# Layer 0's edge stage: one-hots stored in pairs, the running maximum spread between the halves of the weighing, row waits by halves

## The chip, the cores and the metric

The kernel runs on one core of a Trainium2 chip. The metric is the device time of one execution in microseconds (us). Engines are called by their short names in the profile: PE is TensorE (PEld its loading of weights), DVE VectorE, ACT ScalarE, POOL GpSimd, SP SyncE. The granted TensorE clock has two levels, 1.2 and 2.4 GHz; the profile writes it as a share, 0.50 and 1.00.

## What is computed

A graph network of four layers over 6250 nodes of 128 features and 206250 edges. Only layer 0's edges are touched by the change. Cut to that layer:

```python
def _L0_gnn_ref(x, edge_index, W_w, W_b, a_w, a_b):
    h = x @ W_w + W_b
    row, col = (edge_index[0], edge_index[1])
    e = h[row] @ a_src + h[col] @ a_dst + a_b
    e = jax.nn.leaky_relu(e, negative_slope=0.01)
    attention = jax.nn.softmax(e, axis=0)          # over all edges at once
    msg = attention * h[col]
    return jax.ops.segment_sum(msg, row, num_segments=N_NODES)
```

The softmax runs over all edges, so the kernel keeps one running maximum and rescales the sums when it rises.

## The kernel before

The edges are sorted by source and cut into tiles of 128, one edge to a partition; a pair of tiles belongs to one block of 128 nodes. `l0_edges` goes through them in units of 32 tiles (`U`), which fall into two halves of 16 tiles (8 pairs). There are 54 units. The loops over them (one on each engine) have a body of six units. Three row buffers (`R`) take turns; SyncE refills one half at a time once its sums are made (`summed`) and its locations saved (`saved`).

A row has 128 features, a one, the destination's part of the score, the edge's location in its block (column W - 2) and its index. For a unit n, the engines share the work so:

- **VectorE** compares the location with 0..127 (`compare`, L1248), one half of a unit at a time: `sel`, 128 columns of zeros and a one for each tile, in bf16. It works out the scores (`finalize`, from L1255: sum of the three parts, bias, leaky relu, the partition's maximum into `mx`), takes the maximum over the partitions (`raise_max`, L1263 and L1264, into `mrun`), renews the negated maximum (`renew`, L1271 and L1273), multiplies the one-hots by the weights `p` (`weigh`, L1279, two halves, into `oh`, f32), and adds the 16 pair sums to `agg` (`add`, L1290); which block is added to is read from memory into registers, for eight pairs at a time (L1116).
- **TensorE** transposes the one-hots (`turn`, L1179, four groups of eight tiles), multiplies them with the source's score parts (`score`, L1186), turns `mx` (`turn_max`, L1192), spreads `mrun` to all partitions (`spread_out`, L1196), and makes the pair sums (`total`, L1206): 16 f32 multiplies of 129 columns for a half, which the profile shows as 32 records.
- **ScalarE** copies each transposed group out of PSUM (`evacuate`, L1144; there is one such buffer), makes the exponentials (`exponents`, L1148 and L1149), scales `agg` (L1161), and saves locations and indices (L1165, L1166).

All orders are written out by hand. In the step of unit n, VectorE does `weigh(n)` in both halves, `compare` of unit n+2's first half, `raise_max(n+1)`, `compare` of the second half, `renew(n+1)`, `add(n)`, `finalize(n+2)`. TensorE does `turn_max(n+1)`, `total(n)` for the first half, the first `turn` of n+2, `spread_out(n+1)`, half of `total(n)` for the second half, the second `turn`, the first `score`, the other half of the second `total`, and the remaining turns and scores, the last of which releases `finalize(n+2)`. Each engine takes its instructions in this order. There is one buffer of weighed one-hots (`oh`), one place in PSUM for each half's sums (`psA`), and two buffers of `sel`.

## Time and profile before

| | us |
|---|---|
| median of 3 runs | 12102.42 |
| lowest, highest | 12091.43, 12109.16 |
| the profiled execution | 12107.04 |
| its span, first to last instruction | 12105.2 |
| layer 0's edge stage in it, first to last weighing | 3340.3 to 4367.8 |

The whole kernel is a row of stages; the stage that matters here is 1/12 of it. The page's averages over the span say little of it, so the rows below come from questions to the trace about this stretch. In the timeline, rows of one kind that follow each other are merged, and the brackets tell how long the engine stood idle before the row, and what it waited for. "issue" is idle time for which the profile shows no wait.

### The profile page before, as it was taken

To read this page: it belongs to the slowest core of one execution; us is meant where nothing else is said; L and a number is where in the kernel's file an instruction comes from. 1 tells how busy PE (TensorE), PEld (TensorE's weight loads), DVE (VectorE), ACT (ScalarE), POOL (GpSimd) and SP (SyncE) were. 2 spreads that over 40 slices of the span, in tenths; PEclk is the share of its full clock that TensorE was granted. 3 is DMA by queue.
4 is the path that set the end of the run, shared out by engine and by line. 5 is a ranking of instruction groups with operands and counts; after the bars stand their busy time and mean duration, and the time that the engine had idled before them with its cause. 6 is when DMAs were issued, how large, how long until landed. Compare 5 with 4: busy or idle time off the path is not lost. (4 is left out here: it accounts for less than half of the span.)

```text
span 12105.2 us, 161778 instructions
## 1 busy us (share of the span) xinstructions
PE 7567.7 (63%) x46439; PEld 6355.7 (53%) x46440; DVE 6295.9 (52%) x14477; ACT 2657.0 (22%) x4442; POOL 5226.8 (43%) x5267
## 2 busy tenths in 40 slices
PE   3433333333266647777777772999956777777775
PEld 2233333333266645555555552666636777777775
DVE  8722222222277765555555554777764555555555
ACT  4011111111155541111111112444420000000000
POOL 0166666666500016666666662000015555555553
PEclk7766666666677778888888886999975555555555
DMA  4144444443444434444444453000012222233225
GB/s 142 49 126 126 125 126 127 127 125 125 139 109 109 115 101 121 116 123 119 121 124 116 123 112 76 0 0 0 0 36 73 81 80 80 80 82 82 80 81 80
DMA packets 1150557, 1137.58 MB, mean 94 GB/s; under 512 B 239363, under 2 KB 959825, under 8 KB 1150117
## 3 DMA queue, kind: packets, MB, share of 16 engines
q1 hardware_dynamic: 948422, 666.82, 19.0%
q0 software_dynamic: 195904, 465.66, 14.7%
q10 hardware_dynamic: 6048, 2.84, 0.1%
q8 instruction: 93, 1.52, 0.1%
q14 instruction: 90, 0.74, 0.0%
HBM read 731.30 MB, written 403.51 MB: 94 GB/s over the span
## 5 line engine op out<-in xcount | busy, mean ns | idle before, releaser
L1051 POOL DMA_INDIRECT buf<-node_rows,buf x1728 | 1716.9, 994 | 1218.8 <-issue 1033.2
L1545 POOL DMA_INDIRECT buf<-node_rows_ln,buf x1728 | 1751.6, 1014 | 1088.0 <-DVE buf L1672 596.7
L717 POOL DMA_INDIRECT edge_rows_by_src<-buf x1728 | 1695.1, 981 | 1080.8 <-ACT buf L727 537.0
L761 PE MATMUL psum<-buf 128*128 x3456 | 725.5, 377 | 1714.1 <-ACT buf L736 1089.8
L761 PEld LDWEIGHTS psum<-buf 128*128 128x128 f32 x3456 | 656.0, 282 | 1769.9 <-issue 1769.1
L2437 PE MATMUL psum<-buf 128*128 128x132 f32 x3456 | 886.0, 412 | 479.2 <-issue 469.1
L2437 PEld LDWEIGHTS psum<-buf 128*128 128x128 f32 x3456 | 774.0, 309 | 564.5 <-issue 562.9
L2048 PE MATMUL psum<-parts,buf 128*128 x4896 | 917.6, 329 | 99.8 <-DVE buf L2084 44.8
L2429 PE MATMUL psum<-buf 128*128 128x5 f32 x3456 | 754.8, 356 | 164.7 <-ACT buf L2406 83.1
L2429 PEld LDWEIGHTS psum<-buf 128*128 128x128 f32 x3456 | 745.2, 332 | 180.3 <-ACT buf L2406 93.2
L1670 DVE TENSOR_TENSOR buf<-psum,buf 128x512 f32<-128x512 f32 x432 | 298.1, 690 | 1014.6 <-remote 679.2
L2064 DVE TENSOR_TENSOR buf<-buf,ends_of 128x2048 bf16<-128x2048 bf16 x616 | 727.1, 1222 | 124.4 <-issue 120.9
L2026 ACT CAST buf<-psum 128x1024 bf16<-128x1024 f32 x612 | 619.5, 1012 | 693.5 <-PE psum L2037 693.5
L1602 PE MATMUL psum<-buf 128*128 128x512 f32 x864 | 563.0, 739 | 295.5 <-ACT buf L1563 267.9
L809 DVE COPY buf<-buf 128x32 int32<-128x32 int32 x108 | 23.1, 214 | 1368.2 <-DMA buf<-records_by_dst 1127.8
L1560 ACT ACTIVATE buf<-psum 128x512 f32<-128x512 f32 x432 | 258.0, 597 | 2052.3 <-remote 1157.4
L1607 PEld LDWEIGHTS psum<-buf 128*128 128x128 f32 x3456 | 546.3, 224 | 282.8 <-issue 282.8
L2048 PEld LDWEIGHTS psum<-parts,buf 128*128 128x128 bf16 x4896 | 471.9, 96 | 411.6 <-issue 204.4
L2199 POOL IOTA buf<- 49x1 f32 x1 | 0.1, 125 | 1464.1 <-POOLq L844 1464.1
L727 ACT COPY buf<-psum 128x520 f32<-128x520 f32 x432 | 248.9, 595 | 1675.1 <-remote 1217.8
L1615 PE MATMUL psum<-buf 128*128 128x128 f32 x3456 | 518.5, 297 | 132.4 <-DVE buf L1672 101.1
L1206 PE MATMUL psum<-buf 128*128 128x129 f32 x3456 | 538.2, 324 | 100.8 <-DVE buf L1279 100.8
(430 smaller groups left out, 13911.4 us busy)
## 6 DMA issues: line engine op xcount, KB each, us to landing
buf<-edge_rows_by_src SPq DMA_DIRECT2D x114, 1056.0 KB, 5.7
buf<-edge_rows_by_src SPq DMA_DIRECT2D x110, 1024.0 KB
buf<-in_edge_attr SPq DMA_DIRECT2D x864, 128.0 KB
running_weighted_sums<-buf SPq DMA_DIRECT2D x108, 544.0 KB
buf<-loc_rows_by_src SPq DMA_DIRECT2D x110, 512.0 KB
buf<-loc_rows_by_dst SPq DMA_DIRECT2D x110, 512.0 KB
running_sums<-buf SPq DMA_DIRECT2D x108, 512.0 KB
edge_rows_by_src<-buf SPq DMA_DIRECT2D x139, 260.0 KB, 2.8
```

Source lines behind the costliest of these rows:

```text
L717: nc.gpsimd.indirect_dma_start(rows, bass.IndirectOffsetOnAxis(ap=at[:, h, t:t + 1], axis=0), st[:, h, t, :], None).then_inc(scattered[h], 16)
L761: last = nc.tensor.matmul(psX[:, g % 2, t // 2, (t % 2) * WT:(t % 2 + 1) * WT], ohT[:, g % 2, t * P:(t + 1) * P], flat(tab[:, bass.ds(bloc ...
L1051: nc.gpsimd.indirect_dma_start(rows[:, t, 0:used], None, table, bass.IndirectOffsetOnAxis(ap=stage[:, t:t + 1], axis=0)).then_inc(sem, 16)
L1206: last = nc.tensor.matmul(psA[:, half, q // 3, (q % 3) * W:(q % 3) * W + D + 1], oh[:, t, :], rows[:, s, t, 0:D + 1], start=(k == 0), stop ...
L1545: nc.gpsimd.indirect_dma_start(xn[:, j, t, :], None, table1, bass.IndirectOffsetOnAxis(ap=stage[:, j // 4, at:at + 1], axis=0)).then_inc(g ...
L1602: nc.tensor.matmul(psH[:, 0], w1[:], sT[:, j % 2], start=True, stop=True).then_inc(h_ps, 1)
L1607: last = nc.tensor.matmul(psT[:, (j + 1) % 2, t * P:(t + 1) * P], hS[:, (j + 1) % 2, t * P:(t + 1) * P], w2[:], start=True, stop=True)
L2026: nc.scalar.copy(meets[:, h % 2].rearrange("p a k -> p (a k)"), psM[:, h % 2].rearrange("p a k -> p (a k)")).then_inc(moved, 1)
L2048: last = nc.tensor.matmul(psO[:, h // 2, 0:3 * XW], meets[:, h % 2, k, :], parts[:, bass.ds(blocks[k], 1), :, :].rearrange("p b w d -> p ( ...
L2064: last = nc.vector.tensor_tensor(to[:, b], bc(iota[:].unsqueeze(1), [P, U // 2, P, 2]), bc(ends_of[:, w, at].rearrange("p (a t) -> p a t", ...
L2429: last = nc.tensor.matmul(psS[:, q, :], oh[:, s, 2 * q + k, :], sel[:, b, 2 * q + k, :], start=(k == 0), stop=(k == 1))
L2437: last = nc.tensor.matmul(sums(q), oh[:, h, 2 * q + k, :], rows[:, h, 2 * q + k, :], start=(k == 0), stop=(k == 1))
```

## The change

It touches `l0_edges` alone.

1. `sel`, `oh` and `iota` are stored with two tiles interleaved: [.., pair, 128, 2] and no longer [.., tile, 128]. Transposes and sums read one tile as every second element. A new instruction on VectorE (`pick`, L1251 of the kernel after) copies 16 locations at a time into a bf16 array `locs`, and `compare` takes its locations from there, in pairs, so all its operands are bf16. `weigh` reads `p` in pairs.
2. VectorE's order in a step is now: first half of `weigh(n)`, `raise_max(n+1)`, second half, `renew(n+1)`, then `pick` and `compare` twice, then `add` and `finalize`.
3. TensorE spreads the maximum ahead of all sums of the unit. The second half sum is cut into 3 and 5 pairs, not 4 and 4, and the first 3 tell VectorE (`partly`) that they are made; `add` waits for the rest before its fourth pair.
4. Each half of a row buffer has a semaphore of its own.

```diff
-        rows, oh = sb([P, R, U, W]), sb([P, U, P])
-        sel, turned_sel = sb([P, 2, U, P], BF16), sb([P, GROUPS_U, TURN, P], BF16)
-        iota, ident = sb([P, P], BF16), sb([P, P], BF16)
+        rows, oh = sb([P, R, U, W]), sb([P, U // 2, P, 2])
+        sel, turned_sel = sb([P, 2, U // 2, P, 2], BF16), sb([P, GROUPS_U, TURN, P], BF16)
+        iota, ident, locs = sb([P, P, 2], BF16), sb([P, P], BF16), sb([P, 2, U], BF16)
...
-                        act.wait_ge(got[u % R], 64 * i + 32 * (u // R) + 32)
                         for half in range(2):
+                            act.wait_ge(got[u % R][half], 32 * i + 16 * (u // R) + 16)
...
-                        last = nc.tensor.transpose(psT[:, t, :], sel[:, k, TURN * g + t, :], ident[:])
+                        at = TURN * g + t
+                        last = nc.tensor.transpose(psT[:, t, :], sel[:, k, at // 2, :, at % 2], ident[:])
...
-                            last = nc.tensor.matmul(psA[:, half, q // 3, (q % 3) * W:(q % 3) * W + D + 1], oh[:, t, :], rows[:, s, t, 0:D + 1],
+                            last = nc.tensor.matmul(psA[:, half, q // 3, (q % 3) * W:(q % 3) * W + D + 1], oh[:, t // 2, :, t % 2], rows[:, s, t, 0:D + 1],
...
                     if whole:
                         turn_max(n + 1)
+                        spread_out(n + 1)
                         total(n, s, 0, range(PAIRS))
                     turn(n + 2, k, 0)
                     blocks = blocks_of(ENG.PE, first_pair)
                     if whole:
-                        spread_out(n + 1)
-                        total(n, s, 1, range(PAIRS // 2))
+                        total(n, s, 1, range(3))
                     turn(n + 2, k, 1)
                     score(n + 2, 0, blocks)
                     if whole:
-                        total(n, s, 1, range(PAIRS // 2, PAIRS))
+                        total(n, s, 1, range(3, PAIRS))
...
+                def pick(n, half, k, s, halves_at):
+                    dve.wait_ge(got[s][half], halves_at)
+                    of = slice(half * HALF, (half + 1) * HALF)
+                    nc.vector.tensor_copy(locs[:, k, of].unsqueeze(2), rows[:, s, of, W - 2:W - 1]).then_inc(picked, 1)
+
+                def compare(n, half, k, weighed=None):
+                    dve.wait_ge(picked, 2 * n + (half + 1))
                     if weighed is not None:
                         dve.wait_ge(weighted, 2 * weighed + (half + 1))
...
+                    nc.vector.tensor_tensor(sel[:, k, of], bc(iota[:].unsqueeze(1), [P, PAIRS, P, 2]), bc(by_two(locs[:, k, half * HALF:(half + 1) * HALF]), [P, PAIRS, P, 2]),
                                             ALU.is_equal).then_inc(hot, 1)
...
+                    nc.vector.tensor_tensor(oh[:, at], sel[:, k, at], bc(by_two(p[:, k, of]), [P, PAIRS, P, 2]), ALU.mult).then_inc(weighted, 1)
...
-                        dve.wait_ge(summed, 2 * n + (half + 1))
                         for q in range(PAIRS):
+                            if q == 0 and half == 1:
+                                dve.wait_ge(partly, n + 1)
+                            elif q == 3 * half:
+                                dve.wait_ge(summed, 2 * n + (half + 1))
...
-                        weigh(n, u % 2)
-                        compare(0, u % 2, (u + 2) % R, rows_at, n)
+                        halves_at = 32 * i + 16 * ((u + 2) // R + 1)
+                        weigh(n, u % 2, 0)
                         raise_max(n + 1)
-                        compare(1, u % 2, (u + 2) % R, rows_at, n)
+                        weigh(n, u % 2, 1)
                         renew(n + 1)
+                        for half in range(2):
+                            pick(n + 2, half, u % 2, (u + 2) % R, halves_at)
+                            compare(n + 2, half, u % 2, n)
                         add(n, i * (4 * R * PAIRS) + 2 * u * PAIRS, i * (4 * R * PAIRS) + 2 * u * PAIRS)
```

How it moves instructions, first on VectorE, in the loop's second unit, from the weighing on. ISA and REGISTER_ALU are steps of the engine's sequencer. Before:

```order
L1279 TENSOR_TENSOR buf<-buf 128x2048 x2
L1244 REGISTER_ALU
L1246 ISA
L1248 TENSOR_TENSOR buf<-buf 128x2048
L1263 TENSOR_REDUCE buf<-psum 1x1
L90 REGISTER_ALU
L1264 TENSOR_TENSOR buf<-buf 1x1
L1246 REGISTER_ALU
L1248 TENSOR_TENSOR buf<-buf 128x2048
```

And after (L1289 is the weighing, L1273 and L1274 the maximum, L1281 and L1283 the renewal, L1251 the new copy, L1258 the comparison):

```order
L1289 TENSOR_TENSOR buf<-buf 128x2048
L1273 TENSOR_REDUCE buf<-psum 1x1
L90 REGISTER_ALU
L1274 TENSOR_TENSOR buf<-buf 1x1
L1289 TENSOR_TENSOR buf<-buf 128x2048
L1281 TENSOR_SCALAR buf<-buf 128x1
L1282 REGISTER_ALU
L1283 TENSOR_SCALAR buf<-psum 128x1
L1249 REGISTER_ALU
L1251 CAST buf<-buf 128x16
L1254 ISA
L1256 ISA
```

The maximum stands between the weighings, and the comparison comes behind the renewal, with a copy and a wait of its own ahead of it.

On TensorE, at the head of the step of a unit within the loop, L1192 turns the maximum, L1196 spreads it, L1206 are the sums and L1179 the transposes. Before:

```order
L1192 MATMUL psum<-buf 1x128
L1206 MATMUL psum<-buf 128x129 x16
L1176 ISA
L1177 REGISTER_ALU
L1179 MATMUL psum<-buf 128x128 x8
L1116 ISA
L1116 TENSOR_LOAD buf
L1196 MATMUL psum<-buf 128x1
L1206 MATMUL psum<-buf 128x129 x8
```

After (L1194, L1198, L1208 and L1181 in the same roles):

```order
L1194 MATMUL psum<-buf 1x128
L1198 MATMUL psum<-buf 128x1
L1208 MATMUL psum<-buf 128x129 x16
L1177 ISA
L1178 REGISTER_ALU
L1181 MATMUL psum<-buf 128x128 x8
L1116 ISA
L1116 TENSOR_LOAD buf
L1208 MATMUL psum<-buf 128x129 x6
```

The spread moved from behind the first transposes to ahead of the first sum, and the sum behind the transposes has six multiplies for eight.

## Rows read from the trace of the kernel before

**Rows 1.** The weighing, L1279, by line: count, durations in ns, idle time before it

```profile
L1279 DVE TENSOR_TENSOR buf<-buf x108: 2281/2284/2293, 3340.3 to 4367.8; 128x2048 f32<-128x2048 bf16 x108
...
  issue: 25.1, 8
```

**Rows 2.** Groups by line and shape, 3340 to 4366 us: busy us, mean ns | idle

```profile
L1290 DVE TENSOR_TENSOR agg<-agg,psum 128x129 f32 x848 | 246.9, 291 | 194.4 <-issue 54.4 <-DVE agg L1290 36.7
L1248 DVE TENSOR_TENSOR buf<-buf 128x2048 bf16<-128x2048 bf16 x106 | 242.6, 2289 | 0.0
...
L1179 PE MATMUL psum<-buf 128*128 128x128 bf16 x1696 | 129.8, 219 | 49.0 <-ACT buf L1144 49.0
```

**Rows 3.** Timeline, one unit: start us, duration us, engine, line, names, [idle]

```profile
3747.57 4.48 DVE L1279 TENSOR_TENSOR buf<-buf 128x2048 f32<-128x2048 bf16 x2
...
3749.90 5.47 PE L1206 MATMUL psum<-buf 128*128 128x129 f32 x32 [1.83 <-DVE buf L1279]
3751.97 2.29 DVE L1248 TENSOR_TENSOR buf<-buf 128x2048 bf16<-128x2048 bf16 x1
...
3754.47 0.15 DVE L1264 TENSOR_TENSOR buf<-buf 1x1 f32<-1x1 f32 x1
3754.57 2.29 DVE L1248 TENSOR_TENSOR buf<-buf 128x2048 bf16<-128x2048 bf16 x1
...
3755.21 0.61 PE L1179 MATMUL psum<-buf 128*128 128x128 bf16 x8
...
3755.75 0.38 PE L1196 MATMUL psum<-buf 1*128 1x1 f32 x2
...
3756.05 2.05 PE L1206 MATMUL psum<-buf 128*128 128x129 f32 x16
...
3756.96 0.16 DVE L1273 TENSOR_SCALAR buf<-psum 128x1 f32<-128x1 f32 x1
...
3757.98 3.33 DVE L1290 TENSOR_TENSOR agg<-agg,psum 128x129 f32 x8 [0.86 <-issue]
...
3762.11 2.46 DVE L1290 TENSOR_TENSOR agg<-agg,psum 128x129 f32 x6 [0.80 <-DVE agg L1290]
...
3763.99 0.61 PE L1186 MATMUL psum<-buf 128*128 x8 [1.02 <-ACT buf L1144]
...
3765.49 0.25 DVE L1255 TENSOR_REDUCE buf<-psum 128x32 f32<-128x96 f32 x1
3765.61 5.69 ACT L1161 ACTIVATE agg<-agg,buf 128x6468 f32<-128x6468 f32 x1 [1.76 <-DVE agg L1290]
```

**Rows 4.** Timeline, the unit after it

```profile
3766.41 4.48 DVE L1279 TENSOR_TENSOR buf<-buf 128x2048 f32<-128x2048 bf16 x2
...
3768.75 6.25 PE L1206 MATMUL psum<-buf 128*128 128x129 f32 x32 [1.82 <-DVE buf L1279]
...
3780.98 3.32 DVE L1290 TENSOR_TENSOR agg<-agg,psum 128x129 f32 x8 [0.66 <-DVE agg L1290]
...
3783.62 0.62 PE L1186 MATMUL psum<-buf 128*128 x8 [1.02 <-ACT buf L1144]
3784.28 0.26 DVE L1255 TENSOR_REDUCE buf<-psum 128x32 f32<-128x96 f32 x1
```

**Rows 5.** Busy time by window: us, PE, PEld, DVE, ACT, POOL, PEclk, DMA, GB/s

```profile
3753.20:3755.30 2.10, 2.10 (x21) 2.09 (x20) 2.07 (x4) 0.00 (x0) 0.00 (x0) 0.97 0.00 0
3772.20:3773.70 1.50, 1.50 (x9) 1.50 (x9) 1.47 (x4) 0.00 (x0) 0.00 (x0) 0.50 0.00 0
```

**Rows 6.** Layer 2's comparison, L2064, by line: min/median/max ns

```profile
L2064 DVE TENSOR_TENSOR buf<-buf,ends_of x616: 1216/1222/1227, 7558.4 to 8862.4; 128x2048 bf16<-128x2048 bf16 x154
```

**Rows 7.** Loading of block numbers by VectorE's sequencer, L1116: min/median/max ns

```profile
L1116 DVEq TENSOR_LOAD <-buf x108: 594/600/881, 3349.9 to 4379.1; - x108
```

**Rows 8.** Timeline, the first comparison of the stage

```profile
3312.71 4.49 DVE L1248 TENSOR_TENSOR buf<-buf 128x2048 bf16<-128x2048 bf16 x2 [4.98 <-DMA buf<-edge_rows_by_src]
```

**Rows 9.** Layer 2's multiplies of bf16 one-hots in pairs, L2037: min/median/max ns

```profile
L2037 PE MATMUL psum<-buf x4904: 217/218/314, 7560.8 to 8862.4; 128*128 128x128 bf16 x197
```

More of the change, by code:

```diff
@@ L1306, in _ @@
                 renew(0, again=False)
-                compare(0, 1, 1, 32)
-                compare(1, 1, 1, 32)
+                for half in range(2):
+                    pick(1, half, 1, 1, 16)
+                    compare(1, half, 1)
                 finalize(1, 1, 1)
```

39 lines of the change are left out of this document (19 added, 20 removed).

## Prediction

> **What bounds the kernel now.** Only layer 0's edge stage is edited, so I read that stage alone. The weighing's row gives its borders: the first weighing starts at 3340.3, the 108th at 4367.8 us [rows 1]. That is 54 units with two weighings each; the last unit starts one weighing (2.2) before 4367.8, so 53 periods fill 4365.6 - 3340.3 = 1025.3 us, 19.35 each. Eight of them cross the end of the loop's body of six units; there VectorE stands for 25.1 us in all [rows 1]. The rest is (1025.3 - 25.1) / 53 = 18.87 us for a unit.
>
> The groups by line say what VectorE does in a unit: two weighings of 2.28, two comparisons of 2.29, sixteen additions of 0.29 [rows 2]. The timeline of one unit then shows which wait ends last. I count from the start of its weighing, 3747.57 [rows 3]. TensorE's first half sum (below: T0) starts at 2.33, when the first weighed half is ready, and takes 5.47. Then come eight transposes, the spread of the maximum (L1196), half of the second sum, and so on in a row to the last scores, which end at 3764.60, or 17.03. VectorE goes weigh, weigh, compare, maximum, compare, renew (ends 3757.12), 0.86 us of loading block numbers, eight additions, 0.80 us of the same, eight additions. `finalize` follows them without idle time, at 3765.49, or 17.92. So in this unit VectorE is last, and TensorE's chain has ended 0.89 us earlier.
>
> The next unit [rows 4] starts at 3766.41 and reads differently: T0 takes 6.25, the scores end at 3784.24 (17.83), the additions at 3784.30 (17.89). Both chains end together. The cause is TensorE's clock: in the first unit it is at 0.97 from 3753.2 on, 3.3 us after T0 began; in the second it is still at 0.50, the lower of the two levels, up to 3773.7, 4.95 us after T0 began [rows 5]. The two sorts take turns nearly throughout: by T0's length 28 of the 54 units are long (5.9 or more) and 26 short. **The point of the whole case:** VectorE is the bound by 0.9 us in every other unit and by nothing in the others.
>
> From finalize's start to the next weighing it is 0.92 (3765.49 to 3766.41), and finalize starts about 0.05 after the last scores where it waits for them. TensorE's chain alone would thus give a period of 17.03 + 0.97 = 18.00 in the short sort, 17.83 + 0.97 = 18.80 in the long one.
>
> **VectorE's side of the change.** Each comparison becomes all bf16, in pairs. The same form stands in layer 2: 128x2048 bf16 in 1222 ns [rows 6], against 2289 [rows 2]. Two of them: -2.13 us. Added are two copies of 16 location values. The nearest rows are VectorE's one-element 0.16 (L1273) and small L1264, 0.15 [rows 3]; with the comparison's wait for each I take 0.3 each, +0.6. The block numbers' load, 594 to 600 ns [rows 7], and the 0.86 us around it follow the renewal's 0.16 us instruction today; behind the second comparison (1.22 us) they are hidden: -0.8. If that cover is absent, 0.8 comes back, still below TensorE's end. The weighing stays a mix of bf16 and f32; I leave it at 2.28.
> New chain: weighing 2.20, maximum 0.40, weighing 2.20 (the steps in [rows 3]: 4.40 for the pair, 2.60 for comparison and maximum), renewal 0.35, copies and comparisons 0.6 + 2.4, so 8.15 instead of 10.41 for the first addition. From there to finalize it was 7.5 (3757.98 to 3765.49), so VectorE could be there at 15.65 and have a period near 16.6: 2.2 us less. Were VectorE alone, that is 54 x 2.2 = 119 us.
>
> **TensorE's side.** T0 now stands behind the spread of the maximum, and that waits for the maximum, which follows the first weighing. The first weighing is done at 2.20, L1264 ends 0.45 later (it ends at 3754.62, and the comparison ahead of it gave way at 3751.97 + 2.20 = 3754.17), TensorE needs 0.05 to see it, and from the spread to the next sum it is 0.30 (3755.75 to 3756.05) at full clock, some 0.1 more at the low one. T0 starts at 3.0 to 3.1 and not at 2.33: +0.7. In return the spread leaves the place between transposes and second sum: these are 0.84 apart now (3755.21 to 3756.05), eight transposes alone cost about 0.45, so -0.4. T0's first multiply also finds its weights loaded behind the spread, which may give up to 0.15. Net +0.3, bounds +0.1 and +0.5. The 3+5 split of the second half sum adds no work. The first transposes of the new unit need a comparison done at about 6.7, as late as today (3751.97 + 2.29 = 6.69) and before T0's end near 8.5. The first additions now wait for T0 (8.5 or 9.3), and end at 16.1 or 16.9: 1.2 us before the scores (17.3 or 18.1). The wait at the fourth addition for the whole second half costs nothing then. ScalarE's scaling of agg (5.69 us, from 3765.61) starts earlier and stays hidden. SyncE's loads follow `summed` and `saved` as before.
> So **the wait that goes (finalize on the additions) is replaced by another one (finalize on the scores)**. Period: 18.0 + 0.3 = 18.3 in a short unit, 18.8 + 0.3 = 19.1 in a long one, mean 18.7. With a less favourable low-clock stretch I take 18.75, 0.1 below the 18.87 of now: 54 x 0.1 = -5 us. TensorE's quiet time ahead of T0 is 4.1 us in every unit (0.97 + 3.1); today it is 4.1 or 3.3 and the clock is at 0.50 at T0's start in both sorts, so I expect no unit without the drop.
>
> **Start of the stage.** The first comparison waits for both halves of the rows (4.98 us of idle time [rows 8]); now for one. The four turns behind it are paced by ScalarE, so only the first comparison's 1.07 less 0.3 counts, twice: -1.5, and perhaps 0.5 for the earlier half. -2 us. The loop's crossings (25.1 us) stay.
>
> **Stride.** The sums now read their f32 weights from every second element, the transposes theirs in bf16. Layer 2 multiplies such bf16 operands at 218 ns [rows 9], the transposes here take 219 [rows 2]: nothing. No row has f32 weights at such a step. I take nothing; the bound is a rival below.
> The Trainium skill, page "SBUF — State Buffer", section "Door 1: The DMA port swizzle", says that SBUF is read at full bandwidth while at least two accesses fall on one line of 16 bytes. f32 at every second element has exactly two, so by it the sum is unchanged, while one less would make this change slower. No run here shows it yet.
>
> **Sum.** -5 - 2 = -7 us on the profiled execution's 12107.0 (span 12105.2), so 12100. That execution is 4.6 us above the median of the three runs, 12102.4; the same -7 on the median is 12095.5.
>
> **Rivals.**
> (a) The low clock lasts long in every unit. T0 starts later against the clock's rise, and all units are of the long sort or longer: 19.1 to 19.4, so 0.25 to 0.5 x 54 = +13 to +28 us. It decides from a T0 of 6.2 us in nearly every unit. For it: units with 6.25 exist and TensorE now has no slack to hide them. Against: short units exist as well and the period hardly moves. 0.12, half of that past 0.2%.
> (b) f32 weights at a step of two load slower. At full clock a record of T0's kind takes 2.05 / 16 = 0.13 us; if loading took twice as long as the stream, 64 records a unit cost up to 0.1 us more each, 6.4 x 54 = +350 us. It shows as a longer mean of the sums' multiplies than now. For it: no row covers the form. 0.08.
> (c) Short units in a row: 18.3 each, 0.55 x 54 = -30 us. Needs the clock's rise to fall well in every unit. 0.08.
> (d) The clock stays up between units, so T0 takes 4.1 (twice 2.05), TensorE's period is 18.3 - 1.4 = 16.9, and VectorE's gain comes through: -1.9 x 54 = -100 us. Against it: 3.3 us of quiet lose the clock today. 0.05.
> (e) The comparison does not get faster (form not taken at two elements a cycle). VectorE's period is then 16.6 + 2.1 = 18.7: no more than TensorE's mean, +5 us. 0.03.
>
> **How the numbers follow.** My forecast has 0.64, plus (e) and half of (a) that stay within 0.2% (24 us, about what a measurement of this kernel can tell from no change): same 0.72. Faster: (d) 0.05, (c) 0.08 and a little of the forecast's fast edge, 0.14. Slower: (b) 0.08 and half of (a), 0.14. The range takes in the forecast's bounds (net +0.1 to +0.5 on 54 units, 11 us to either side), all of (a) and most of (c): 12068 to 12128; (b) and (d) stay out.
>
> **What would show it.** After the change the comparison should read near 1220 ns, the block load's gap ahead of the first addition be gone, replaced by a wait for the sums; finalize's first reduction should be preceded by an idle time of 1 us or so put down to the scores; T0 should start 3.0 to 3.1 after the weighing. The forecast is wrong if T0's length no longer takes turns between 5.4 and 6.3, or if multiplies of the sums grow.

## Result and the profile after

| | before | after |
|---|---|---|
| median, us | 12106.33 (18 runs, 12078.97 to 12125.2) | 12129.01 (18 runs, 12109.82 to 12163.96) |
| ratio, 95% interval | | 1.0017 (1.001 to 1.0024) |
| the profiled execution, its span | 12107.04, 12105.2 | 12109.82, 12107.9 |
| first weighing to the last unit's start | 1025.2 | 1053.3 |

The changed kernel takes 22.7 us more by the medians. The forecast was 7 us less. 12129.0 also lies just outside the range that ended at 12128; 3.9 us of it come from the kernel before, whose median was 12102.4 over three runs and is 12106.3 over 18.

The two profiled executions differ by 2.7 us only, and this is no contradiction. The weighing of the kernel after, by line (count, durations in ns, idle time before it), gives the stage's borders:

```profile
L1289 DVE TENSOR_TENSOR buf<-buf x108: 2272/2278/2293, 3326.1 to 4382.0; 128x2048 f32<-128x2048 bf16 x108
...
  issue: 26.4, 8
```

It begins at 3326.1 where before it began at 3340.3 [rows 1], and ends 14.2 later than before, not earlier. The last unit begins one weighing and the maximum (2.58) before 4382.0, so 53 periods fill 1053.3 us: 28.1 more than before. Of the 14.2 us by which the start is earlier, 8.7 come from stages that the change doesn't touch: `l0_edges` clears `agg` that much earlier. The other 5.5 are the stage's own opening, from this clearing to the first weighing, 38.05 us before and 32.51 after. The clearing before, then after:

```profile
3302.29 5.45 DVE L1298 MEMSET agg<- 128x6468 f32 x1 [1.28 <-issue]
```

```profile
3293.60 5.45 DVE L1311 MEMSET agg<- 128x6468 f32 x1 [1.28 <-issue]
```

28.1 more in the units and 5.5 less in the opening make 22.6, which fits the 22.7 by the medians. The experiments below ran in three sets, each with its own runs of the kernel before. In two of them the first weighing falls between 3297.5 and 3313.6, in the third (`e5`, `e7`, `e8`, `e9`) between 2802.9 and 2808.9. So from here on I measure the stage alone, by its 53 periods. "Period" is the time from a unit's first weighing to the next one's, averaged over the 45 units that do not cross the end of the loop's body. It was 18.82 and is 19.27; the eight crossings were 22.27 each and are 23.25. 45 x 0.45 + 8 x 0.98 = 28.1.

The eight crossings rose by more than the other periods, and I come back to that at the end. Groups of the kernel after in this stretch (busy us, mean ns | idle before):

```profile
L1208 PE MATMUL psum<-buf 128*128 128x129 f32 x3424 | 556.8, 333 | 0.0
...
L1303 DVE TENSOR_TENSOR agg<-agg,psum 128x129 f32 x864 | 251.6, 291 | 249.0 <-PE psum L1208 102.2 <-DVE agg L1303 29.7 <-issue 9.2
...
L1258 DVE TENSOR_TENSOR buf<-buf 128x2048 bf16<-128x2048 bf16 x106 | 129.9, 1225 | 6.8
...
L1198 PE MATMUL psum<-buf 1*128 1x1 f32 x106 | 30.8, 357 | 122.4 <-DVE buf L1274 122.4
...
L1251 DVE CAST buf<-buf 128x16 bf16<-128x16 f32 x106 | 18.0, 169 | 0.0
L1265 DVE TENSOR_REDUCE buf<-psum 128x32 f32<-128x96 f32 x54 | 13.9, 258 | 69.1 <-PE psum L1188 69.1
```

VectorE did what was asked of it: the comparison fell from 2289 [rows 2] to 1225 ns, the new copy costs 169. The additions' "issue" idle time fell from 54.4 to 9.2 us, so the load of block numbers ahead of the first addition is covered now; 102.2 us of waiting for the sums came in its place. And `finalize` (L1265), which followed the additions, now stands idle for 69.1 us in 54 units, all put down to the last scores. VectorE's gain went into those two waits.

Now one unit, the counterpart of [rows 3], with T0 of the short sort. The timeline of the kernel after:

```profile
3763.44 2.28 DVE L1289 TENSOR_TENSOR buf<-buf 128x2048 f32<-128x2048 bf16 x1
...
3765.94 0.15 DVE L1274 TENSOR_TENSOR buf<-buf 1x1 f32<-1x1 f32 x1
...
3766.15 0.58 PE L1198 MATMUL psum<-buf 1*128 1x1 f32 x2 [2.20 <-DVE buf L1274]
...
3766.66 5.44 PE L1208 MATMUL psum<-buf 128*128 128x129 f32 x32
...
3771.93 0.61 PE L1181 MATMUL psum<-buf 128*128 128x128 bf16 x8
...
3772.38 1.63 PE L1208 MATMUL psum<-buf 128*128 128x129 f32 x12
3772.41 3.33 DVE L1303 TENSOR_TENSOR agg<-agg,psum 128x129 f32 x8 [1.14 <-PE psum L1208]
...
3774.50 2.60 PE L1208 MATMUL psum<-buf 128*128 128x129 f32 x20
...
3776.94 0.61 PE L1181 MATMUL psum<-buf 128*128 128x128 bf16 x8
...
3780.47 0.64 PE L1188 MATMUL psum<-buf 128*128 x8 [1.02 <-ACT buf L1145]
3781.15 0.26 DVE L1265 TENSOR_REDUCE buf<-psum 128x32 f32<-128x96 f32 x1 [1.43 <-PE psum L1188]
```

Counted from the weighing's start, the last scores end at 17.67; in the short unit before it was 17.03. VectorE is ready 1.43 us before them. The unit ahead of it is of a sort that the kernel before hardly had (one T0 above 6.6 in 54). Its T0, and the same two waits:

```profile
3743.56 2.28 DVE L1289 TENSOR_TENSOR buf<-buf 128x2048 f32<-128x2048 bf16 x1
...
3746.78 6.72 PE L1208 MATMUL psum<-buf 128*128 128x129 f32 x32
...
3753.80 3.33 DVE L1303 TENSOR_TENSOR agg<-agg,psum 128x129 f32 x8 [2.44 <-PE psum L1208]
...
3762.50 0.26 DVE L1265 TENSOR_REDUCE buf<-psum 128x32 f32<-128x96 f32 x1 [1.03 <-PE psum L1188]
```

T0 takes 6.72, against 5.44 and, in [rows 4], 6.25. The windows of the kernel after (us, busy time of PE, PEld, DVE, ACT, POOL, then PEclk) show that this is the clock:

```profile
3747.00:3752.50 5.50, 5.50 (x26) 5.50 (x27) 4.26 (x7) 0.89 (x5) 0.00 (x0) 0.50 0.01 3
3752.90:3753.30 0.40, 0.40 (x6) 0.40 (x5) 0.00 (x0) 0.00 (x0) 0.00 (x0) 1.00 0.00 0
3766.70:3769.70 3.00, 3.00 (x15) 3.00 (x15) 2.93 (x5) 1.06 (x5) 0.00 (x0) 0.50 0.02 5
3769.90:3771.90 2.00, 2.00 (x19) 2.00 (x19) 1.34 (x3) 0.00 (x0) 0.00 (x0) 1.00 0.00 0
```

In the long unit the lower level holds for more than 5.7 us of T0, in the short one for some 3.1. TensorE is busy throughout in both. The lengths of T0 in a row were 5.4 and 6.3 in turn; now they are 5.4, 6.3, 6.75 in turn, with periods of 18.6, 19.45 and 19.95. What TensorE did ahead of T0 does not decide between the three: from the last scores to the next T0 it is 4.2 us, with the turned maximum and its spread in it, in every unit but the first of a body. Of 54 T0s, 28 took 5.9 or more before, 36 do now; the mean went from 5.89 to 6.18.

### The profile page after: what moved, and what is told of

It reads as the page before. It is cut to its first block and busy times, and to the rows that moved or that the text cites. A ratio compares the mean times of both kernels' runs of the same rounds, so it can differ in the third digit from the quotient of the medians.

```text
span 12107.9 us, 162000 instructions
## 1 busy us (share of the span) xinstructions
PE 7652.0 (63%) x46439; PEld 6434.5 (53%) x46440; DVE 6182.2 (51%) x14589; ACT 2652.6 (22%) x4442; POOL 5234.1 (43%) x5267
## 5 line engine op out<-in xcount | busy, mean ns | idle before, releaser
L2081 DVE TENSOR_TENSOR buf<-buf,ends_of 128x2048 bf16<-128x2048 bf16 x616 | 727.1, 1222 | 111.5 <-issue 111.5
```

The costliest lines, as they stand in the source:

```text
L2081: last = nc.vector.tensor_tensor(to[:, b], bc(iota[:].unsqueeze(1), [P, U // 2, P, 2]), bc(ends_of[:, w, at].rearrange("p (a t) -> p a t", ...
```

## Experiments

The theory (A in the expectations): VectorE's gain can't be used because `finalize` now waits for the last scores, and TensorE's chain has become longer by two things: T0 stands behind the maximum and its spread, and the sums read their f32 weights at a step of two. The rivals: that the order alone, or the pairs alone, costs the 28 us; that T0's later start makes the clock's low stretch longer by itself; that a wait on VectorE is the cause. H in the expectations adds to the theory that the part of T0 at the low clock grows in steps as the chain grows. For each kernel the time of its stage (53 periods), the mean period and the mean of T0 stand in one table at the end of this section. The stage of each is from one profile; the changed kernel, profiled in two sets, gave 1053.3 and 1055.0 us, and the kernel before was profiled once. The intervals of the whole-kernel ratios are some 10 us wide to either side or more, so differences of a few us are read from the stage.

### Each half of the change alone

`e1_pairs_alone` keeps the pairs and has the order of before on both engines:

```diff
                         turn_max(n + 1)
-                        spread_out(n + 1)
                         total(n, s, 0, range(PAIRS))
...
-                        total(n, s, 1, range(3))
+                        spread_out(n + 1)
+                        total(n, s, 1, range(PAIRS // 2))
...
                         weigh(n, u % 2, 0)
+                        weigh(n, u % 2, 1)
+                        pick(n + 2, 0, u % 2, (u + 2) % R, halves_at)
+                        compare(n + 2, 0, u % 2, n)
                         raise_max(n + 1)
-                        weigh(n, u % 2, 1)
+                        pick(n + 2, 1, u % 2, (u + 2) % R, halves_at)
+                        compare(n + 2, 1, u % 2, n)
                         renew(n + 1)
...
```

> The changed kernel with one part alone: tiles in pairs, the copy of the locations and the faster comparison, but VectorE and TensorE in the order of before (spread behind the first transposes, sums of 4 and 4 pairs). Theory A (TensorE's chain from the first half sum T0 to the last scores sets the unit, VectorE was the bound only in short units): T0 starts at 2.34 us after the weighing as before, the comparisons at 1.22 gain VectorE 2 us of which it can use none in long units, and reading f32 weights at a step of two costs TensorE 6 ns a record at full clock (0.118 for 0.112 in the changed kernel's trace), some 0.25 us a unit. Mean period 18.6 to 18.9, time within 10 us of before. Rival B (VectorE is the bound and the pairs are what matters): period 16.9 to 17.5, 70 to 100 us under before.

`e2_order_alone` has the new order and the layout and comparison of before:

```diff
-        rows, oh = sb([P, R, U, W]), sb([P, U // 2, P, 2])
-        sel, turned_sel = sb([P, 2, U // 2, P, 2], BF16), sb([P, GROUPS_U, TURN, P], BF16)
-        iota, ident, locs = sb([P, P, 2], BF16), sb([P, P], BF16), sb([P, 2, U], BF16)
+        rows, oh = sb([P, R, U, W]), sb([P, U, P])
+        sel, turned_sel = sb([P, 2, U, P], BF16), sb([P, GROUPS_U, TURN, P], BF16)
+        iota, ident = sb([P, P], BF16), sb([P, P], BF16)
...
-                    of = slice(half * PAIRS, (half + 1) * PAIRS)
-                    nc.vector.tensor_tensor(sel[:, k, of], bc(iota[:].unsqueeze(1), [P, PAIRS, P, 2]), bc(by_two(locs[:, k, half * HALF:(half + 1) * HALF]), [P, PAIRS, P, 2]),
+                    of = slice(half * HALF, (half + 1) * HALF)
+                    nc.vector.tensor_tensor(sel[:, k, of, :], bc(iota[:].unsqueeze(1), [P, HALF, P]), bc(rows[:, s, of, W - 2:W - 1], [P, HALF, P]),
```

> The other part alone: the changed kernel's order on VectorE and TensorE and its semaphores, but tiles one after the other, comparisons in f32 locations at 2.29 us, no copy of locations. Theory A: T0 starts at 3.2 as in the changed kernel, because it stands behind the spread; VectorE is 1.8 us later than there, still at or before the scores in long units; no cost of stride, so TensorE's chain is 0.25 shorter. Mean period 18.9 to 19.2, 5 to 20 us over before, at or up to 15 us under the changed kernel. Rival B: losing the comparison's gain shows in full, period 20.5 or more, 80 us and more over before.

Measured: 1.0005 (0.9994 to 1.0016) and 1.0011 (1.0001 to 1.002). The stages took 1028.3 and 1029.1, so 3 and 4 us more than before; together the parts cost 28. The period of the first, 18.92, lies just over what was expected, that of the second, 18.85, just under. The medians are 12 and 19 us over before. For the second, whose interval is 1 to 24 us, the profile shows less: 3.9 more in the periods and 3.6 less in the opening. Where the rest of its 19 us lies was not found. The groups of `e1_pairs_alone`, then of `e2_order_alone`:

```profile
L1208 PE MATMUL psum<-buf 128*128 128x129 f32 x3456 | 557.7, 330 | 97.4 <-DVE buf L1287 97.4
...
L1299 DVE TENSOR_TENSOR agg<-agg,psum 128x129 f32 x864 | 251.5, 291 | 199.8 <-issue 53.1 <-PE psum L1208 27.0 <-DVE agg L1299 11.9
```

```profile
L1208 PE MATMUL psum<-buf 128*128 128x129 f32 x3456 | 536.8, 324 | 0.0
...
L1258 DVE TENSOR_REDUCE buf<-psum 128x32 f32<-128x96 f32 x54 | 13.9, 258 | 43.0 <-PE psum L1188 42.9
```

With the pairs alone the 53 us of "issue" ahead of the additions are still there, since the short renewal still precedes them; the sums' multiplies take 330 ns in the mean for 324. With the order alone they take 324, and the wait for the scores is there, with 43 us. In `e2_order_alone` TensorE's scores end 0.45 later than before (17.93 for 17.48 in the mean), and the period grows by 0.03: the 0.45 is what `finalize` stood behind the scores before, in the mean of all units. In `e1_pairs_alone` they end 0.36 later (17.84). Neither part alone is the cause, and neither is free for TensorE: each fills the slack.

### T0 early again

`e3_spread_inside` starts T0 ahead of the spread; with it the renewal, which needs the spread, moves behind the comparisons. The rest is the changed kernel:

```diff
                         turn_max(n + 1)
+                        total(n, s, 0, range(4))
                         spread_out(n + 1)
-                        total(n, s, 0, range(PAIRS))
+                        total(n, s, 0, range(4, PAIRS))
...
-                        renew(n + 1)
                         for half in range(2):
...
                             compare(n + 2, half, u % 2, n)
+                        renew(n + 1)
```

> The changed kernel with the spread of the maximum moved from ahead of T0 to its middle, behind four of its eight pairs, and the renewal behind the comparisons. Theory A: T0 starts at 2.34 again, the spread costs 0.3 to 0.5 inside it, so the chain is 0.4 to 0.5 us shorter than the changed kernel's; mean period 18.6 to 18.9, 15 to 30 us under the changed kernel and within 10 us of before. Rival C (the new waits on VectorE, copy and partly, are what costs): no change against the changed kernel, period 19.2 to 19.4, 20 us over before.

Measured: 0.9999 (0.999 to 1.0007), stage 1023.9. T0 starts at 2.34 and not at 3.22, and with the spread inside it takes 6.52; it thus ends at 8.86, after 9.40 in the changed kernel. Of the 0.88 that it starts earlier, 0.54 reach its end, and the period falls by 0.42. Without the late T0 the loss is gone, though every wait that the change put on VectorE is still there: the late T0 is a necessary part of it. It is not a sufficient one, as `e2_order_alone` shows.

### The stride

`e10_flat_by_reads` is the changed kernel with `oh` stored tile by tile. The weighing reads the pairs at a step of two and writes in a row, so that the sums' weights are contiguous:

```diff
-        rows, oh = sb([P, R, U, W]), sb([P, U // 2, P, 2])
+        rows, oh = sb([P, R, U, W]), sb([P, U, P])
...
-                    nc.vector.tensor_tensor(oh[:, at], sel[:, k, at], bc(by_two(p[:, k, of]), [P, PAIRS, P, 2]), ALU.mult).then_inc(weighted, 1)
+                    nc.vector.tensor_tensor(oh[:, of, :].rearrange("p (a t) j -> p a t j", t=2), sel[:, k, at].rearrange("p a j t -> p a t j"), bc(p[:, k, of].rearrange("p (a t) -> p a t", t=2).unsqueeze(3), [P, PAIRS, 2, P]), ALU.mult).then_inc(weighted, 1)
```

> As the flat weighed one-hots, but the weighing walks tile after tile: it writes 2048 f32 in a row and reads the bf16 one-hots at a step of two (in the run before, it wrote alternately to two tiles 512 bytes apart, and took 3.74 us for 2.28). Theory A with a cost of stride on TensorE: weighing back at 2.28 us, records of the sums 0.112 us apart, period 18.8 to 19.0, time 10 to 25 us under the changed kernel, 0 to 12 us over before. Rival F (the stride is not what costs): period stays at 19.2 to 19.4, 20 us over before. If reading at a step of two is slow as well, the weighing stays above 3 us and the time above before by 60 us or more.

Measured: 1.0007 (0.9995 to 1.002), stage 1030.6, period 18.98. The sums' group and the weighing by line:

```profile
L1208 PE MATMUL psum<-buf 128*128 128x129 f32 x3456 | 537.6, 324 | 0.0
```

```profile
L1289 DVE TENSOR_TENSOR buf<-buf x108: 2271/2278/2293, 3304.0 to 4337.2; 128x2048 f32<-128x2048 bf16 x108
```

The multiplies are back at 324 ns, and T0's mean falls from 6.18 to 5.93. Only the stride of the sums' weights is gone, and 22.7 of the 28.1 us go with it. (The medians alone could not show it: 1.0007 and the changed kernel's 1.0025, in another set, have intervals that overlap.) At full clock the stride costs 6 ns a record: the 20 records of the second half sum take 2.60 in the changed kernel (above), and 2.48 in the contiguous `e11_quarters_by_reads` (below), and 12 take 1.63 and 1.56. At the half clock the records are 0.214 to 0.218 apart with the stride and without (distances of single records within T0). The 22.7 us are 0.43 a unit. Behind T0 a unit has 32 records, 32 x 6 ns = 0.19, and from the second sum to the third group of transposes it is 4.56 with the stride and 4.36 without, so 0.20; T0's mean is 0.25 longer. At 6 ns a record T0's part at full clock, 19 records in the short sort and 6 in the longest, explains at most 0.1 of that. The other 0.15 or more is not in the records' distances at either clock; it is the longer low stretch. Laid over the trace's record of the granted clock, T0 has 4.78 us at 0.50 in the changed kernel in the mean, and 4.36 here; the kernel before had 4.28. The long T0s go from 36 back to 29.

### The same delay without the stride

If steps of the clock are what multiplies a small delay, it must not matter where the delay is from. `e12_order_plus_5` is `e2_order_alone` with five multiplies that nothing reads, ahead of the second half sum; `e13_order_plus_10` has ten of them:

```diff
+                def fill(count):
+                    for _ in range(count):
+                        nc.tensor.matmul(psS_[:, 384:512], ident[:], ident[:], start=True, stop=True)
...
                     if whole:
+                        fill(5)
                         total(n, s, 1, range(3))
```

> The run with the order alone (mean period 18.85) with 5 multiplies of 56 ns each between its first transposes and its second half sum, all on TensorE's chain: 0.28 us a unit, about what the stride cost in the changed kernel. Theory H (the share of T0 at the low clock grows with the chain, in steps): the period goes up by more than 0.28, to 19.2 to 19.35 as in the changed kernel, with three lengths of T0 in turn. Theory I (a plain sum): 19.05 to 19.15, T0's mean length as before the addition (5.9).

> The same with 10 multiplies, 0.56 us a unit. Theory H: once in the state with three lengths, the chain adds less than its own length: 19.4 to 19.6. Theory I: 19.35 to 19.45 with T0 at 5.9. The two are told apart by T0's mean length (H: 6.2 or more) and by the run with 5.

Measured in one profile each, so only the stage is compared: 1051.9 and 1070.9 us, periods 19.31 and 19.80. Periods and T0s of the six units of one body of the loop, the sixth, worked out from the weighings and from the first and last records of T0 (the last of the six crosses to the next body):

```
                     period, T0 (us)
e2_order_alone       18.51 5.53 | 19.45 6.49 | 18.32 5.34 | 19.42 6.38 | 18.24 5.25 | 22.24 6.32
e12_order_plus_5     18.83 5.57 | 19.61 6.36 | 20.05 6.78 | 18.60 5.35 | 19.67 6.25 | 22.77 6.64
e13_order_plus_10    19.72 6.18 | 20.07 6.55 | 20.29 6.74 | 18.87 5.19 | 19.50 5.97 | 23.02 6.44
```

Five multiplies add 0.28 us to the chain: a unit with T0 of 5.34 took 18.32, one with 5.35 takes 18.60. The mean period grows by 0.46 and the stage by 22.8 us, 0.43 for each of its 53 periods. The pattern is that of the changed kernel: three lengths in turn, 36 long T0s, stage within 1.4 us of it. The next five add 0.49 to the period where I had expected less than 0.28; counted with the crossings, which fall by 0.4, it is 0.36 for each of the 53, still more than 0.28. 42 T0s are long, and the short one comes less often. T0's part at the low clock is 4.33 us in the mean in `e2_order_alone`, 4.82 with five multiplies and 4.95 with ten. The rows of `e12_order_plus_5`:

```profile
L1208 PE MATMUL psum<-buf 128*128 128x129 f32 x3456 | 549.5, 329 | 0.0
...
L1263 DVE TENSOR_REDUCE buf<-psum 128x32 f32<-128x96 f32 x54 | 13.9, 257 | 64.8 <-PE psum L1188 64.8
```

Here 329 ns is the low clock's larger share, since nothing is strided. So a sum's mean of one duration can't tell a slower instruction from a slower clock; the distance of records at one clock can.

### Without the low stretch

`e4_fillers` is the changed kernel with multiplies that nothing reads, in the places where TensorE waits:

```diff
                         turn_max(n + 1)
+                        fill(30)
                         spread_out(n + 1)
...
+                    if whole:
+                        fill(10)
                     turn(n + 2, k, 3)
                     score(n + 2, 2, blocks)
+                    if whole:
+                        fill(10)
                     score(n + 2, 3, blocks)
```

> The changed kernel with 50 multiplies of 128 bf16 columns a unit that compute nothing, 30 behind the turned maximum, 10 ahead of the fourth group of transposes and 10 ahead of the last scores, all in time that TensorE waits through. Theory D (the low clock at T0 is the price): TensorE is busy for most of the quiet time, the granted clock stays at 1.00 through T0, T0 takes 3.9 to 4.3 us for 6.2, mean period 17.2 to 17.6, 65 to 90 us under before. Rival E (the clock falls all the same, or the fillers only stand in the way): T0 stays near 6 and starts later by up to 0.8 us, period 19.3 to 20, 20 to 60 us over before.

`e7_fillers_on_before` has the same fifty in the kernel before, in the same places:

```diff
                         turn_max(n + 1)
+                        fill(30)
                         total(n, s, 0, range(PAIRS))
...
+                    if whole:
+                        fill(10)
                     turn(n + 2, k, 3)
                     score(n + 2, 2, blocks)
+                    if whole:
+                        fill(10)
                     score(n + 2, 3, blocks)
```

> The kernel before with the same 50 multiplies a unit that compute nothing. The clock stays up, T0 takes 4.1 us, TensorE's chain ends near 15.7. Theory A: VectorE's chain (18.7 with its own order) is then the bound in every unit, so the clock alone is worth little there: mean period 18.5 to 18.8, 0 to 15 us under before, 60 us over the changed kernel with fillers; that is, the change is worth its 60 us only once TensorE does not bind. Rival G (fillers are worth the same on any of the two): 65 to 80 us under before.

Measured: 0.9935 (0.9921 to 0.9949), 68 us less than before, against 0.9993 (0.9984 to 1.0002). The timeline and a window of `e4_fillers`:

```profile
3711.91 2.28 DVE L1298 TENSOR_TENSOR buf<-buf 128x2048 f32<-128x2048 bf16 x1
3712.05 0.27 PE L1194 MATMUL psum<-buf 128*1 128x128 f32 x1 [1.11 <-DVE buf L1277]
3712.16 1.84 PE L1217 MATMUL psum<-buf 128*128 128x128 bf16 x30
...
3714.62 0.38 PE L1198 MATMUL psum<-buf 1*128 1x1 f32 x2 [0.62 <-DVE buf L1283]
3714.92 4.04 PE L1208 MATMUL psum<-buf 128*128 128x129 f32 x32
```

```profile
3714.90:3718.90 4.00, 4.00 (x35) 3.97 (x36) 3.90 (x7) 1.46 (x5) 0.00 (x0) 1.00 0.00 0
```

The clock is at 1.00 all through T0, which takes 4.04; L1217 are the fillers. So it is in 45 of the 54 units. In 33 of them T0 starts at 3.01, as here; in the other 21 units it starts at 3.3 to 5.5, the thirty fillers ahead of it taking longer, and lasts at most 4.83; the mean start is 3.45. Here the spread takes 0.38 and T0 starts at 3.01, just where the forecast had it: the 0.2 more in the changed kernel are the spread at the low clock. The stage takes 957.9, the one of `e7_fillers_on_before` 1014.1. In the groups of `e7_fillers_on_before` `finalize` hardly waits for the scores (7.4 us in all), so the additions are last:

```profile
L1206 PE MATMUL psum<-buf 128*128 128x129 f32 x3413 | 449.1, 290 | 1.4 <-DVE buf L1288 1.3
...
L1264 DVE TENSOR_REDUCE buf<-psum 128x32 f32<-128x96 f32 x54 | 13.5, 251 | 7.4 <-PE psum L1186 7.4
```

With fillers in both kernels the change is thus worth 56 us of the stage, 1.06 a period. The prediction's 2.2 us a unit don't come through in full because TensorE is still last (`finalize` waits 57.9 us for the scores in `e4_fillers`).

### Towards a faster kernel

`e9_changed_again` is the changed kernel without an edit, for the comparison with the two that went with it.

> The changed kernel once more, on the chip of these runs, so that the flat weighed one-hots can be set against it. All theories: 15 to 28 us over before, mean period 19.2 to 19.4, T0 in cycles of three lengths.

1.0025 (1.0014 to 1.0036), in a set of runs in which the rest of the kernel is shorter (before: 10349.2); its stage takes 1055.0. `e5_flat_weighed` and `e8_quarters_fillers` take the stride out on the other side, in what the weighing writes; the second also halves the first weighing, starts T0 behind a quarter and fills the waits:

```diff
-                    nc.vector.tensor_tensor(oh[:, at], sel[:, k, at], bc(by_two(p[:, k, of]), [P, PAIRS, P, 2]), ALU.mult).then_inc(weighted, 1)
+                    nc.vector.tensor_tensor(oh[:, of, :].rearrange("p (a t) j -> p a j t", t=2), sel[:, k, at], bc(by_two(p[:, k, of]), [P, PAIRS, P, 2]), ALU.mult).then_inc(weighted, 1)
```

> The changed kernel with the weighed one-hots (f32) stored tile after tile again, so that the sums read their weights at a step of one; the unweighed ones stay in pairs and the comparison stays at 1.22 us. Theory A with a cost of stride: records of the sums are 0.112 us apart at full clock again (0.118 in the changed kernel), TensorE's chain is 0.2 to 0.3 us shorter, and because with that the low clock covers T0 less often the unit loses more than that: mean period 18.8 to 19.0 as in the run with the order alone, 10 to 20 us under the changed kernel. Rival F (the stride costs only its own 0.25 us, or nothing): 19.0 to 19.3, at most 12 us under it.

```diff
-                        weigh(n, u % 2, 0)
+                        weigh(n, u % 2, 0, PAIRS // 2)
+                        weigh(n, u % 2, PAIRS // 2, PAIRS // 2)
                         raise_max(n + 1)
-                        weigh(n, u % 2, 1)
-                        renew(n + 1)
+                        weigh(n, u % 2, PAIRS, PAIRS)
...
+                        ahead = blocks_of(ENG.DVE, i * (4 * R * PAIRS) + 2 * u * PAIRS)
+                        renew(n + 1)
+                        add(n, ahead, i * (4 * R * PAIRS) + 2 * u * PAIRS, i * (4 * R * PAIRS) + 2 * u * PAIRS)
```

> What the runs so far point to, together: the changed kernel with the spread inside T0, flat weighed one-hots, the first half weighed in two quarters so that T0 starts at 1.3 us, block numbers loaded ahead of the renewal, and 30 fillers a unit (10, 10, 10). Theory A: TensorE's chain is 2 us shorter than with fillers alone, VectorE's own chain (16.6 to 17.2) is the bound: mean period 16.7 to 17.3, 90 to 115 us under before. If 30 fillers don't hold the clock, T0 takes over 5 us and the period is 17.3 to 18.0, 45 to 80 us under before.

Both came out slower, 1.0089 (1.0075 to 1.0103) and 1.0046 (1.0032 to 1.006), and both missed what was expected for one reason above all, which the weighing's row in `e5_flat_weighed` shows:

```profile
L1289 DVE TENSOR_TENSOR buf<-buf x108: 3703/3712/3782, 2802.9 to 3918.8; 128x2048 f32<-128x2048 bf16 x108
```

The halves of the first weighing in `e8_quarters_fillers`, by its group:

```profile
L1301 DVE TENSOR_TENSOR buf<-buf 128x1024 f32<-128x1024 bf16 x108 | 205.1, 1979 | 23.5 <-issue 23.5
```

The same number of elements as ever takes 3712 ns for 2278. Successive f32 results go to two tiles in turn, 512 bytes apart. That experiment therefore says nothing about the stride of the sums; `e10_flat_by_reads`, above, was made for it. `e11_quarters_by_reads` is `e8_quarters_fillers` with the weighing of `e10_flat_by_reads`, against the changed kernel:

```diff
-                    nc.vector.tensor_tensor(oh[:, at], sel[:, k, at], bc(by_two(p[:, k, of]), [P, PAIRS, P, 2]), ALU.mult).then_inc(weighted, 1)
...
+                    nc.vector.tensor_tensor(oh[:, of, :].rearrange("p (a t) j -> p a t j", t=2), sel[:, k, at].rearrange("p a j t -> p a t j"), bc(p[:, k, of].rearrange("p (a t) -> p a t", t=2).unsqueeze(3), [P, count, 2, P]), ALU.mult).then_inc(weighted, 1)
```

> The version with spread inside T0, first half weighed in quarters, block numbers ahead of the renewal and 30 fillers, its weighing now writing in a row. Theory A: weighing 1.2, 1.2 and 2.28 us, T0 starts at 1.3, VectorE's chain of 16.6 to 17.2 is the bound if the clock holds: mean period 16.7 to 17.3, 85 to 115 us under before, better than the changed kernel with fillers (68 to 78 under). If 30 fillers do not hold the clock: 17.3 to 18.2, 35 to 75 us under before.

Measured: 0.9915 (0.9897 to 0.9932), 11809.16 against 11905.9: 97 us less than before and the lowest ratio of all kernels here. Its timeline and two of its groups:

```profile
3708.59 2.35 DVE L1301 TENSOR_TENSOR buf<-buf 128x1024 f32<-128x1024 bf16 x2
...
3709.86 3.69 PE L1210 MATMUL psum<-buf 128*128 128x129 f32 x16 [0.30 <-DVE buf L1301]
...
3713.80 2.05 PE L1210 MATMUL psum<-buf 128*128 128x129 f32 x16
...
3716.13 1.56 PE L1210 MATMUL psum<-buf 128*128 128x129 f32 x12
```

```profile
L1301 DVE TENSOR_TENSOR buf<-buf 128x1024 f32<-128x1024 bf16 x108 | 127.0, 1218 | 23.0 <-issue 23.0
...
L1277 DVE TENSOR_REDUCE buf<-psum 128x32 f32<-128x96 f32 x54 | 13.9, 258 | 32.6 <-PE psum L1188 32.3
```

T0 begins 1.27 us after the weighing. Its first 16 records take 3.69, the next 16 take 2.05, so the low clock is back here, with ten fillers ahead of T0; yet the early start wins more. `finalize` still waits for the scores, 32.3 us in all. The period of 17.02 was expected, but with a clock that holds and VectorE as the bound; neither came, so the number is right by luck.

The period here is the mean of the 45 that do not cross, T0 the mean of all 54; "long" is 5.9 or more.

| kernel | stage, us | period | T0's start | T0, mean | long T0s |
|---|---|---|---|---|---|
| before | 1025.2 | 18.82 | 2.34 | 5.89 | 28 |
| after | 1053.3 | 19.27 | 3.22 | 6.18 | 36 |
| e1_pairs_alone | 1028.3 | 18.92 | 2.34 | 6.06 | 28 |
| e2_order_alone | 1029.1 | 18.85 | 3.22 | 5.92 | 29 |
| e3_spread_inside | 1023.9 | 18.85 | 2.34 | 6.52, with the spread | |
| e10_flat_by_reads | 1030.6 | 18.98 | 3.22 | 5.93 | 29 |
| e12_order_plus_5 | 1051.9 | 19.31 | 3.22 | 6.13 | 36 |
| e13_order_plus_10 | 1070.9 | 19.80 | 3.22 | 6.20 | 42 |
| e4_fillers | 957.9 | 17.65 | 3.45 | 4.10 | 0 |
| e5_flat_weighed | 1112.0 | 20.42 | 4.60 | 6.07 | |
| e8_quarters_fillers | 1068.5 | 19.71 | 2.03 | 6.47, with the spread | |
| e9_changed_again | 1055.0 | 19.30 | 3.22 | 6.21 | 36 |
| e7_fillers_on_before | 1014.1 | 18.64 | 3.13 | 4.32 | 0 |
| e11_quarters_by_reads | 925.1 | 17.02 | 1.29 | 5.58, with the spread | |

## Why the prediction was wrong

**What bounds the kernel: held.** VectorE was last by 0.9 us in the short units and by nothing in the long ones. That explains why a chain of TensorE that is 0.45 longer costs 0.03 a unit in `e2_order_alone`.

**VectorE's terms: held.** Comparison 1225 ns (1222 by [rows 6]); the copy 169 ns (0.3 with its wait); the load of the block numbers covered. The additions end 1.0 and 1.4 us before `finalize` starts, as forecast (1.2). The wait of `finalize` for the scores took the place of the one for the additions, as forecast: 69.1 us of it.

**TensorE's terms: here the sum failed.** Net +0.3 with bounds of +0.1 and +0.5 was forecast; the short units show +0.64. Mis-sized were T0's start and the stride. Term by term, the short unit of [rows 3] against the one at 3763.44:

| term | forecast | measured |
|---|---|---|
| T0's start | +0.7 | +0.89 (2.33 to 3.22) |
| weights found loaded behind the spread | 0 to -0.15 | 0 |
| T0, to the transposes | 0 | -0.04 (5.31 to 5.27) |
| spread gone from between transposes and second sum | -0.4 | -0.39 |
| second sum to the third transposes | 0 | +0.15 (4.41 to 4.56): stride +0.20, order -0.05 |
| third transposes to the last scores | 0 | +0.03 |
| sum | +0.3 | +0.64 |

The -0.05 is seen without the stride, in `e2_order_alone` and `e10_flat_by_reads`, where this stretch takes 4.36. The start was mis-sized since I priced the spread at full clock and "some 0.1 more" at the low one; from the spread's start to T0's it is 0.51 here against 0.30, and `e4_fillers`, at full clock, has just the 3.01 that was forecast. The stride was priced at nothing where no row had the form, and its bound went straight to a rival of 350 us: a small price, 6 ns a record, had no place in the sum or in the range.
The Trainium skill, page "SBUF — State Buffer", section "Door 1: The DMA port swizzle", would have f32 at a step of two free, with two accesses on each line of 16 bytes. The rows don't agree: 2.60 against 2.48 us for 20 records at full clock. At the half clock they do (0.214 to 0.218 us between records in both layouts).

**From the unit to the mean: the other half.** I took the short and long sort as fixed and set +0.3 on each, with 0.05 for "a less favourable low-clock stretch". With +0.64 the mix itself changed: T0's mean grew by 0.29, and a sort of 6.75 appeared. Over all 54 units the scores end at 18.39 for 17.48 in the mean: +0.91, of which 0.88 is T0's start, 0.29 its length and -0.26 the rest. `finalize` stood 0.45 behind the scores before and 0.04 now, which hides 0.41; the 0.50 that is left makes 26.5 of the 28.1 us over 53 periods. Set against the forecast's net +0.3, T0's 0.29 is 15 us of the miss and the other terms (0.88 - 0.26 = 0.62 for 0.3) are 17; but the experiments show the first to follow from the second. This is near rival (a), which had 0.12, and its upper end has the size (+28 us for the units; measured 28.1). Its own sign, a T0 of 6.2 us in nearly every unit, came in 36 of 54 only: a third of the units stays short, and half of the long ones are longer than it had them. The range said that it took in all of (a), and didn't: 12128 is the forecast 12100 plus 28, where (a) was priced against the kernel before, 12102.4 + 28 = 12130. `e10_flat_by_reads` tells how near the forecast was to right: without the stride the 53 periods cost 5 us more than before. `e12_order_plus_5` tells that 0.28 us of multiplies throw it over as the stride does. Both halves of the change are needed for the loss, and 28 is not 3 + 4.

**The signs that I had named** (T0's length no longer takes turns between 5.4 and 6.3, the multiplies of the sums grow) both came. **Start and crossings:** the opening of the stage, forecast at -2 us, gained 5.5 (38.05 to 32.51). It repeats: 38.2 in `e7_fillers_on_before`, 32.4 to 32.8 in every kernel with pairs, 34.2 to 34.6 in the three that have the comparison of before but wait for half of the rows. So the half wait is worth some 3.8, priced at 0.5, and the faster comparison some 1.8, priced at 1.5. It is a miss in the favourable direction, and hid a fifth of the loss. The crossings, which I left at their price, rose by 0.98 each, 7.8 us in all. In the eight units that cross, `finalize` starts 0.80 later than before (18.92 for 18.13), with T0 at 6.64 for 5.65; from there to the next weighing it is 0.18 more (4.32 for 4.14). So 0.8 of the 0.98 is the same lengthening, and the 0.18 was not taken apart. Why the lengths of T0 fall into two, three or more values in turn was not settled either; the runs show that they do, and at which delay.

**The sign.** 22.7 us is 0.19% of the time, and the interval (0.10 to 0.24%) leaves out zero, though it lies mostly within the 0.2% that I gave 0.72. The predicted direction, 7 us faster, is excluded. That the change stays so small is no support for the sum: the units moved by 28 us up where 5 down were forecast, and the opening took 5.5 of it back.

## What to carry to other kernels

If two engines end together in some repetitions of a loop, price a change by what it does to the one that will be last, and look at that chain for small additions: here 2.2 us a unit won on one engine were worth nothing, and 0.6 a unit lost on the other cost 28 us over 53 periods. Where the granted clock drops in every repetition, a mean over two sorts of repetition is no base for a sum; ask what a delay of a few tenths does to the mix, and price nothing at the full clock that runs during the drop. Before giving a layout a price of zero because no row has it, put a small price beside it, and try the layout both ways: here VectorE read at a step of two at no cost, and that took the step away from TensorE, which pays for it.

## What the runs showed of the hardware

- A tensor_tensor on VectorE, 128x2048, bf16 times f32 into f32: 2278 ns when it reads the bf16 at a step of two and writes in a row, 2278 when all is interleaved alike, and 3712 when it reads in a row and writes in turn to places 512 bytes apart. With 1024 elements the means are 1218 and 1979 ns. Here the stride costs nothing on the bf16 reads.
- f32 weights at a step of two: 0.118 us between the records of the sums at full clock for 0.112 contiguous, and 0.214 to 0.218 for both at the half clock. The bf16 transposes take 219 ns at a step of two as before [rows 2].
- Fifty multiplies of 128 columns a unit that nothing reads, set where TensorE waits in the changed kernel, give a T0 of 4.04 to 4.83 us for 5.3 to 6.8, and a time 68 us under that of the kernel before. In the kernel before, where VectorE is then last, they change next to nothing (-7.6 us, with zero inside the interval).
- A delay of 0.28 us on the chain that binds moved the stage by 0.43 us a unit, and a second one by 0.36: more than itself, while T0's mean part at the low clock grew from 4.33 to 4.82 to 4.95 us.
- From TensorE's last scores to the next T0 it is 4.2 us in all units but the first of a body of the changed kernel, and T0, which starts at the low clock, still takes 5.4, 6.3 or 6.75 us.
